# The state space stage's norm is scaled by ScalarE, with a bias that GpSimd makes

## The chip, the core and the metric

The kernel is a decoder of four layers (twelve sub-blocks, one after another) that runs as one program on one core of a Trainium2 chip. The metric is the device time of the program in microseconds. The engines' names in the profile are PE (TensorE, matmul), PEld (its weight load), DVE (VectorE), ACT (ScalarE), POOL (GpSimd) and SP (SyncE, DMA queue).

## The reference

The input x has 64 sequences of 64 tokens, 128 wide. Each sub-block adds its result to x. The change lies in the seventh, a state space model on the normalised x (`_L2_attn_ref`), with 256 channels and N = 16 states:

```python
def _layernorm(x, axis=-1, eps=1e-05):
    m = jnp.mean(x, axis=axis, keepdims=True)
    v = jnp.var(x, axis=axis, keepdims=True)
    return (x - m) / jnp.sqrt(v + eps)
...
xr = x @ w_in + b_in
xc, res = jnp.split(xr, 2, axis=-1)
u = jax.nn.silu(_causal_conv(xc, w_conv, b_conv))
A = -jnp.exp(A_log)
dt, B, C = jnp.split(u @ w_x, [DTR, DTR + N], axis=-1)
delta = jax.nn.softplus(dt @ w_dt)
deltaA = jnp.exp(delta[..., None] * A)
deltaBu = delta[..., None] * B[:, :, None, :] * u[..., None]
h = a * h + bu        # over time, for each channel and state
...
y = jnp.einsum('bldn,bln->bld', hs, C) + u * D
return y * jax.nn.silu(res) @ w_out
```

## The kernel before

The stage is `state_space` (line 2336). It works through NG = 8 groups of 512 tokens (8 sequences); group g's x lies as `e.X(g)`, 128 partitions by 4 tiles of 128 columns. After the norm and a transpose, channels are partitions: c = 0 and 1 are the two halves of the 256 channels, tokens are the 512 columns. Inside a group, k = 0 to 15 runs over the states, and m = 16 g + k counts through all of them. Each engine has a program of its own, written out in order; semaphores tie them together, and an engine that waits holds up all that stands behind in its program.

For each m, and each c: ScalarE's `decay` (line 2558, an Exp of 128x504 into PSUM) and `copy_b` (2551, the row of B from PSUM to SBUF), GpSimd's `inputs` (2616, du times that row, 128x512 each), VectorE's `scan` (2681) and then `contribute` (2688, the scan's result times the row of C), and TensorE's `accumulate` (2432) with its rows of B and C (`b_row`, `c_row`). The scan of m needs decay and input product of m; the decay of m + 1 needs the scan of m, since both use one bank. The input products are double-buffered (two m).

Between these, the steps for the groups around are placed by k. At k = 7 VectorE takes the norm's statistics of group g + 2 (`PipedNorm.stats`, 643), at k = 8 GpSimd makes 1/std from them (`rstd`, 656: an add and a power on 128x4), at k = 12 VectorE scales (`PipedNorm.scale`, 665: one TENSOR_SCALAR of 128x128 for each of the four tiles, into the one buffer `xn`). At k = 13 TensorE turns them (`turn`, 2369) and ScalarE copies the result (`copy_ln`, 2488); at k = 14 and 15 follow the input projections. For group g + 1: convolution at k = 0 to 3, at k = 5 to 10 the other projections with SiLU (k = 6), the rows of B and C (`high_part`, `below_high`, and `parts` on GpSimd at k = 9) and the step sizes; ScalarE's `softplus` (k = 11) is an Ln, which needs a table load before it and another one after it for the next Exp. At k = 12 GpSimd's `step_size` (2627) makes delta and du, two products of 128x1024. At k = 1 to 5 the output of group g - 1 is finished: `skipped` (VectorE), `gated` (GpSimd), `output` (TensorE), `residual` (VectorE, 2702). Groups 6 and 7 have no group g + 2, and so no statistics and no scale in the loop.

The norm of groups 0 and 1 and all projections of group 0 are made ahead of the loop, in a serial prologue. There ScalarE's program runs `copy_ln(0)` first, and `copy_ln(1)` right behind `copy_b(1)`.

Of the kernel before, what the change touches and what calls it, by code (L numbers as in the profile page):

```python
# [18 lines left out]
ALU = mybir.AluOpType  # L19
# [5 lines left out]
D = 128  # L25
NT = 4
# [600 lines left out]
NG = 8  # L627


class PipedNorm:  # L630
# [25 lines left out]
    def rstd(self, q, g):  # L656
        rs, mv = self.half(self.rs, g, 2 * NT), self.half(self.mv, g, 2 * NT)
        q.wait_ge(self.mean_s, g + 1)
        if g >= 2:
            q.wait_ge(self.xn_s, NT * (g - 1))  # L660
        q.tensor_scalar(rs[:, 0:NT], tiles(mv)[:, :, 1], self.eps, None, ALU.add).then_inc(self.var_s, 1)  # L661
        q.wait_ge(self.var_s, g + 1)
        q.tensor_tensor(rs[:, NT:2 * NT], rs[:, 0:NT], self.e.mhalf[:, 0:NT], ALU.pow).then_inc(self.rstd_s, 1)  # L663

    def scale(self, q, g):
        rs, mv = self.half(self.rs, g, 2 * NT), self.half(self.mv, g, 2 * NT)
# [1669 lines left out]
def state_space(nc, e, W):  # L2336
# [5 lines left out]
    M = NG * N  # L2342
    use = ssm_order()
    names = PN_SEMS + ("zeroed misc_mm misc_cp taps_done u_done res_done hi_done parts_own bc_parts relu_done sp_own sp_done "
                       "dl_done du_done b_mm c_mm b_cp a_done bu_done hs_done hc_done acc_mm yo_done yr_done")
    with block_of(nc, "state_space", names) as (block, s):
        room = Room(e.arena)
        u_b, res_b, delta_b, du_b = (room.pair(2 * GT) for _ in range(4))
# [10 lines left out]
        misc = e.bank(7)  # L2359
        at, cbank, bbank, acc = (lambda c: e.bank(c)), (lambda m: e.bank(2 + m % 2)), e.bank(4), (lambda c: e.bank(5 + c))  # L2360
        ln = PipedNorm(e, s, room, e.X, lambda g: xn, 1e-5)

        @block.tensor
        def _(pe):
# [119 lines left out]
        def _(a):  # L2484
# [3 lines left out]
            def copy_ln(g):  # L2488
                have("ln", g)
                if g >= 1:  # L2490
                    a.wait_ge(s["misc_mm"], use["m3", g - 1] + 1)
                a.activation(xnT, misc, ACT.Copy).then_inc(s["misc_cp"], 1)

            def channels(c, g):
                have(("m0", "m1")[c], g)
                if g == 0:
                    a.wait_ge(s["zeroed"], 1)
                else:
                    a.wait_ge(s["misc_mm"], use[("cv0", "cv1")[c], g - 1] + 1)
                a.activation(xp(c)[:, :, 3:3 + S], tiles(misc, NB), ACT.Identity,  # L2500
                             bias=W("b_in")[:, c:c + 1]).then_inc(s["misc_cp"], 1)
# [56 lines left out]
            def decay(m, c):  # L2558
                if m < M:
# [5 lines left out]
                    if k == 0:  # L2565
                        a.wait_ge(s["dl_done"], g + 1)
                    a.activation(tiles(at(c), NB)[:, :, 1:S], tiles(delta(g, c), NB)[:, :, 1:S], ACT.Exp,  # L2567
                                 scale=e.aneg[:, c * N + k:c * N + k + 1]).then_inc(s["a_done"], 1)

            copy_ln(0)  # L2570
            channels(0, 0)
            channels(1, 0)
# [9 lines left out]
            decay(0, 0)  # L2582
            decay(0, 1)
            copy_b(1)
            copy_ln(1)
            channels(0, 1)
            channels(1, 1)
            for m in range(M):
                g, k = m // N, m % N
                decay(m + 1, 0)  # L2590
                copy_b(m + 2)
                decay(m + 1, 1)
                if g + 1 < NG:
                    if k in (1, 3):
                        raw(("cv0", "cv1")[k // 2], g + 1)
                    if k in (5, 6):
                        raw(("m2", "m3")[k - 5], g + 1)
                    if k == 6:
                        silus(g + 1)
                    if k == 7:  # L2600
                        copy_dt(g + 1)
                    if k == 8:
                        high_part(g + 1)
                    if k in (9, 10):
                        step_size(k - 9, g + 1)
                    if k == 11:
                        softplus(g + 1)
                if g + 2 < NG:
                    if k == 13:
                        copy_ln(g + 2)  # L2610
                    if k in (14, 15):
                        channels(k - 14, g + 2)

        @block.gpsimd
        def _(q):
# [36 lines left out]
                q.tensor_copy(low, rest).then_inc(s["bc_parts"], 1)  # L2652
                q.wait_ge(s["bc_parts"], g + 1)

            ln.rstd(q, 0)
            ln.rstd(q, 1)
            parts(0, "ln_rstd", 2)
            step_size(0)
            inputs(0)
            for m in range(M):  # L2660
                g, k = m // N, m % N
                inputs(m + 1)
                if k == 2 and g >= 1:
                    gated(g - 1)
                if k == 12 and g + 1 < NG:
                    step_size(g + 1)
                if k == 9 and g + 1 < NG:
                    parts(g + 1, "bu_done", 2 * (m + 2))
                if k == 8 and g + 2 < NG:
                    ln.rstd(q, g + 2)  # L2670
            gated(NG - 1)

        @block.vector
        def _(v):
# [28 lines left out]
                v.wait_ge(s["misc_mm"], use["y", g] + 1)  # L2703
                v.tensor_tensor(e.X(g), misc, e.X(g), ALU.add).then_inc(s["misc_cp"], 1)

            def scale(g):
                if g >= 1:
                    v.wait_ge(s["misc_mm"], use["ln", g - 1] + 1)
                ln.scale(v, g)

            for c in range(2):
                v.memset(tiles(at(c), NB)[:, :, 0:1], 0.0)
            v.memset(xp_all, 0.0).then_inc(s["zeroed"], 1)
            ln.stats(v, 0)
            ln.stats(v, 1)
            scale(0)
            for c in range(2):
                for i in range(4):
                    ins = v.tensor_scalar(taps(c, i), e.ident, W("w_conv")[:, 4 * c + i:4 * c + i + 1], None, ALU.mult)
            ins.then_inc(s["taps_done"], 1)  # L2720
            scale(1)
            below_high(0)
            for m in range(M):
                g, k = m // N, m % N
# [7 lines left out]
                    below_high(g + 1)  # L2732
                scan(m, 1)
                contribute(m, 0)
                if g + 2 < NG:
                    if k == 7:
                        ln.stats(v, g + 2)
                    if k == 12:
                        scale(g + 2)
            contribute(M - 1, 1)  # L2740
            skipped(NG - 1)
            residual(NG - 1)
# [1086 lines left out]
```

## Time and profile before

| what | us |
|---|---|
| median of 3 runs | 3444.28 (3443.8 to 3452.95) |
| the profiled execution | 3446.75 |
| its span in the trace | 3444.8 |
| the state space stage in it, first memset to last residual | 1612.6 to 2226.2 |
| VectorE busy, whole kernel | 1954.5 (57% of the span) |
| TensorE / ScalarE / GpSimd busy, whole kernel | 2755.0 / 1330.5 / 1425.9 |

The profile is of one execution. The page gives each engine's busy time over the whole kernel; since the twelve stages differ, the stage is read from stretches of the trace. A timeline row gives start, duration, engine, line, instruction, operands and shapes; a row with x4 merges four neighbours; square brackets hold the idle time of the engine before it and what ended it. The name given there is inferred: where several were waited for, it is the last by the profile.

### The profile page before, as it was taken

Reading aid. Unit: us, or ns where it says so; the run is one execution under the profiler, and the core shown is the slowest. Engines: PE = TensorE matmul, PEld = TensorE weight load, DVE = VectorE, ACT = ScalarE, POOL = GpSimd, SP = SyncE. Lnnn points to the kernel's source line nnn. Section 1 sums busy time; section 2 is a strip of 40 time slices with the busy share of each in tenths; the row PEclk is TensorE's granted clock in tenths of the full one; section 3 lists DMA queues with packets and bytes.
Section 4 is the critical chain, followed back from the end, with each engine's and each line's share of the span. In section 5 each row is a group of like instructions: output and inputs, shape, how many; then the busy total and the mean of one; then the engine's idle time right before and its main releaser. Section 6 shows DMA issues by size and latency. Waiting matters only on the chain. (4 is left out here: it accounts for less than half of the span.)

```text
span 3444.8 us, 72909 instructions
## 1 busy us (share of the span) xinstructions
PE 2755.0 (80%) x28239; PEld 1918.5 (56%) x28239; DVE 1954.5 (57%) x4206; ACT 1330.5 (39%) x2252; POOL 1425.9 (41%) x1537
## 2 busy tenths in 40 slices
PE   4987784998999979786778888695777999993394
PEld 2654453996777755564233333253446888883394
DVE  2654554115767646633599898845565665644123
ACT  3432221441111124321666666352233666651153
POOL 2544443223212145253577777633452111113555
PEclk8988876999999999798899999896788999995697
DMA  6000001660000010033000000000000000001275
GB/s 230 2 1 1 1 1 43 172 175 13 3 3 3 3 46 14 1 115 121 0 1 0 1 1 0 1 1 1 1 2 11 7 7 5 5 2 45 91 230 158
DMA packets 98053, 130.50 MB, mean 38 GB/s; under 512 B 31088, under 2 KB 76528, under 8 KB 97264
## 3 DMA queue, kind: packets, MB, share of 16 engines
q1 hardware_dynamic: 82768, 109.30, 10.5%
q0 software_dynamic: 7168, 14.78, 1.2%
q8 instruction: 227, 3.72, 0.4%
q10 hardware_dynamic: 7776, 1.77, 0.2%
q14 instruction: 114, 0.93, 0.1%
HBM read 103.64 MB, written 25.35 MB: 37 GB/s over the span
## 5 line engine op out<-in xcount | busy, mean ns | idle before, releaser
L661 POOL TENSOR_SCALAR arena<-arena 128x4 f32<-128x4 f32 x120 | 27.5, 229 | 1044.4 <-DVE arena L653 794.1
L2625 POOL TENSOR_TENSOR arena<-arena 128x512 f32<-128x512 f32 x256 | 319.1, 1270 | 141.9 <-ACT arena L2556 141.2
L2686 DVE TENSOR_TENSOR_SCAN arena<-ps,arena 128x512 f32<-128x512 f32 x256 | 312.1, 1219 | 41.3 <-ACT ps L2567 22.5
L2438 PE MATMUL ps<-arena,const_w 128*128 128x512 f32 x512 | 279.2, 629 | 12.6 <-DVE arena L2694 11.5
L163 PEld LDWEIGHTS ps<-L_attn_w,arena 128*128 128x128 f32 x1984 | 241.7, 193 | 53.6 <-issue 42.5
L163 PE MATMUL ps<-L_attn_w,arena 128*128 128x128 f32 x1984 | 257.9, 281 | 8.0 <-POOL arena L2638 3.4
L2567 ACT ACTIVATE ps<-arena,aneg 128x504 f32<-128x504 f32 x256 | 174.4, 681 | 120.0 <-DVE arena L2686 119.8
L1765 PE MATMUL ps<-arena,L_attn_w 128*128 128x512 f32 x384 | 184.5, 617 | 0.9 <-ACT arena L725 0.9
L429 ACT ACTIVATE arena<-ps 128x1024 f32<-128x1024 f32 x96 | 98.3, 1024 | 223.9 <-PE ps L331 223.9
L1833 ACT ACTIVATE arena<-ps,L_attn_w 128x512 f32<-128x512 f32 x64 | 44.0, 687 | 332.6 <-PE ps L1765 332.6
L2694 DVE TENSOR_TENSOR arena<-arena,ps 128x512 f32<-128x512 f32 x256 | 170.0, 665 | 0.0
L312 PE MATMUL ps<-arena 64*64 64x512 f32 x768 | 119.2, 695 | 62.9 <-POOL arena L485 62.9
L2416 PE MATMUL ps<-bcp,sel 96*128 96x512 bf16 x256 | 92.2, 396 | 87.6 <-DVE arena L2694 67.1
L2438 PEld LDWEIGHTS ps<-arena,const_w 128*128 128x128 f32 x512 | 95.0, 198 | 99.6 <-DVE arena L2694 55.1
L423 ACT ACTIVATE arena<-arena 128x1024 f32<-128x1024 f32 x96 | 101.3, 1055 | 96.3 <-DVE arena L551 96.3
L345 PEld LDWEIGHTS ps<-arena 128*64 128x64 f32 x3072 | 108.5, 149 | 49.6 <-issue 27.6
L2229 DVE TENSOR_REDUCE arena<-arena 128x8 f32<-128x512 f32 x128 | 87.2, 681 | 84.1 <-ACT arena L2116 84.0
L2416 PEld LDWEIGHTS ps<-bcp,sel 96*128 96x128 bf16 x256 | 25.5, 100 | 195.2 <-issue 194.2
L485 POOL TENSOR_TENSOR arena<-arena,const_w 128x1024 f32<-128x1024 f32 x64 | 120.6, 1896 | 32.7 <-PE ps L319 22.9
L163 PE MATMUL ps<-L_attn_w,ct_all 128*128 128x128 f32 x1024 | 131.0, 280 | 1.9 <-DVE arena L2245 1.9
L663 POOL TENSOR_TENSOR arena<-arena,mhalf 128x4 f32<-128x4 f32 x120 | 125.4, 1045 | 10.0
L1076 DVE SCALAR_TENSOR_TENSOR arena<-ps,arena 128x64 f32 x108 | 30.7, 284 | 174.2 <-PE ps L895 165.7
(454 smaller groups left out, 6730.7 us busy)
## 6 DMA issues: line engine op xcount, KB each, us to landing
arena<-zone_w SPq DMA_DIRECT2D x54, 512.0 KB
arena<-pair_w SPq DMA_DIRECT2D x40, 578.0 KB
arena<-rt SPq DMA_DIRECT2D x24, 384.0 KB
pair_in<-pair_free SPq DMA_DIRECT2D x1, 5200.0 KB, 28.8
arena<-pair_in SPq DMA_DIRECT2D x40, 130.0 KB
arena<-ctx SPq DMA_DIRECT2D x16, 256.0 KB, 2.9
arena<-pair_out SPq DMA_DIRECT2D x16, 256.0 KB, 5.0
arena<-arena SPq DMA_DIRECT2D x108, 32.0 KB, 2.2
```

Source lines behind the costliest of these rows:

```text
L163: ins = pe.matmul(out, src[:, j * P:(j + 1) * P], w, start=(i == 0), stop=(bias is None and i == len(chunks) - 1))
L312: ins = pe.matmul(tile(b2, h), q(g)[rows, t:t + S], kbd(i)[rows, :, b2 * S:(b2 + 1) * S], start=True, stop=rope)
L345: ins = pe.matmul(obank[b2 * S:(b2 + 1) * S, hp], pts(i)[:, hp * P + b2 * S:hp * P + (b2 + 1) * S], vbd(g)[:, 2 * j + b2, hp], start=True, ...
L485: p_.tensor_tensor(kbd(i), repeat(k(g)[:, j * P:(j + 1) * P], HH), spread(e.hmask8, P), ALU.mult).then_inc(s["kbd_done"], 1)
L663: q.tensor_tensor(rs[:, NT:2 * NT], rs[:, 0:NT], self.e.mhalf[:, 0:NT], ALU.pow).then_inc(self.rstd_s, 1)
L1765: pe.matmul(e.bank(i), W(w)[:, col], xnT(g), start=True, stop=True).then_inc(s["qkg_mm"], 1)
L2416: return pe.matmul(out, e.sel[:, row:row + 1].broadcast_to([96, P]), bcp(g), start=True, stop=True)
L2438: pe.matmul(acc(c), e.ident, hc(m, c), start=(k == 0), stop=(k == N - 1)).then_inc(s["acc_mm"], 1)
L2567: a.activation(tiles(at(c), NB)[:, :, 1:S], tiles(delta(g, c), NB)[:, :, 1:S], ACT.Exp, scale=e.aneg[:, c * N + k:c * N + k + 1]).then_inc ...
L2625: q.tensor_tensor(bu(m, c), du(g, c), bs(m), ALU.mult).then_inc(s["bu_done"], 1)
L2686: v.tensor_tensor_scan(hs(m, c), at(c), bu(m, c), 0.0, ALU.mult, ALU.add).then_inc(s["hs_done"], 1)
L2694: v.tensor_tensor(hc(m, c), hs(m, c), cbank(m), ALU.mult).then_inc(s["hc_done"], 1)
```

## The change

VectorE's `scale` is gone from the stage. `PipedNorm.offset` is new: GpSimd multiplies mean and 1/std (128x4) and negates the product, each step waiting for the one before; it is called right behind each `rstd`. `PipedNorm.scale_act` is new: ScalarE computes x * rs + nb, an Identity activation of 128x128 for each tile with scale and bias from SBUF. Calls stand on ScalarE ahead of `copy_ln(0)`, behind `copy_b(1)`, and at k = 12 for group g + 2, behind the decays of the next k. The statistics stay on VectorE. In the changed file lines are shifted; TensorE's program is the same.

```diff
--- before.py
+++ after.py
@@ -662,6 +662,23 @@
         q.wait_ge(self.var_s, g + 1)
         q.tensor_tensor(rs[:, NT:2 * NT], rs[:, 0:NT], self.e.mhalf[:, 0:NT], ALU.pow).then_inc(self.rstd_s, 1)
 
+    def offset(self, q, g, nb, raw, sem):
+
+        rs, mv = self.half(self.rs, g, 2 * NT), self.half(self.mv, g, 2 * NT)
+        q.wait_ge(self.rstd_s, g + 1)
+        if g >= 2:
+            q.wait_ge(self.xn_s, NT * (g - 1))
+        q.tensor_tensor(nb, tiles(mv)[:, :, 0], rs[:, NT:2 * NT], ALU.mult).then_inc(raw, 1)
+        q.wait_ge(raw, g + 1)
+        q.tensor_scalar(nb, nb, -1.0, None, ALU.mult).then_inc(sem, 1)
+        q.wait_ge(sem, g + 1)
+
+    def scale_act(self, a, g, nb):
+        rs = self.half(self.rs, g, 2 * NT)
+        for j in range(NT):
+            a.activation(self.dst(g)[:, j * self.step:j * self.step + D], self.src(g)[:, j * D:(j + 1) * D], ACT.Identity,
+                         bias=nb[:, j:j + 1], scale=rs[:, NT + j:NT + j + 1]).then_inc(self.xn_s, 1)
+
     def scale(self, q, g):
         rs, mv = self.half(self.rs, g, 2 * NT), self.half(self.mv, g, 2 * NT)
         q.wait_ge(self.mean_s, g + 1)
@@ -2342,7 +2359,7 @@
     M = NG * N
     use = ssm_order()
     names = PN_SEMS + ("zeroed misc_mm misc_cp taps_done u_done res_done hi_done parts_own bc_parts relu_done sp_own sp_done "
-                       "dl_done du_done b_mm c_mm b_cp a_done bu_done hs_done hc_done acc_mm yo_done yr_done")
+                       "nb_raw nb_done dl_done du_done b_mm c_mm b_cp a_done bu_done hs_done hc_done acc_mm yo_done yr_done")
     with block_of(nc, "state_space", names) as (block, s):
         room = Room(e.arena)
         u_b, res_b, delta_b, du_b = (room.pair(2 * GT) for _ in range(4))
@@ -2359,6 +2376,7 @@
         misc = e.bank(7)
         at, cbank, bbank, acc = (lambda c: e.bank(c)), (lambda m: e.bank(2 + m % 2)), e.bank(4), (lambda c: e.bank(5 + c))
         ln = PipedNorm(e, s, room, e.X, lambda g: xn, 1e-5)
+        nb = room.pair(NT)
 
         @block.tensor
         def _(pe):
@@ -2491,6 +2509,12 @@
                     a.wait_ge(s["misc_mm"], use["m3", g - 1] + 1)
                 a.activation(xnT, misc, ACT.Copy).then_inc(s["misc_cp"], 1)
 
+            def scale(g):
+                a.wait_ge(s["nb_done"], g + 1)
+                if g >= 1:
+                    a.wait_ge(s["misc_mm"], use["ln", g - 1] + 1)
+                ln.scale_act(a, g, nb(g))
+
             def channels(c, g):
                 have(("m0", "m1")[c], g)
                 if g == 0:
@@ -2567,6 +2591,7 @@
                     a.activation(tiles(at(c), NB)[:, :, 1:S], tiles(delta(g, c), NB)[:, :, 1:S], ACT.Exp,
                                  scale=e.aneg[:, c * N + k:c * N + k + 1]).then_inc(s["a_done"], 1)
 
+            scale(0)
             copy_ln(0)
             channels(0, 0)
             channels(1, 0)
@@ -2582,6 +2607,7 @@
             decay(0, 0)
             decay(0, 1)
             copy_b(1)
+            scale(1)
             copy_ln(1)
             channels(0, 1)
             channels(1, 1)
@@ -2606,6 +2632,8 @@
                     if k == 11:
                         softplus(g + 1)
                 if g + 2 < NG:
+                    if k == 12:
+                        scale(g + 2)
                     if k == 13:
                         copy_ln(g + 2)
                     if k in (14, 15):
@@ -2652,8 +2680,9 @@
                 q.tensor_copy(low, rest).then_inc(s["bc_parts"], 1)
                 q.wait_ge(s["bc_parts"], g + 1)
 
-            ln.rstd(q, 0)
-            ln.rstd(q, 1)
+            for g in range(2):
+                ln.rstd(q, g)
+                ln.offset(q, g, nb(g), s["nb_raw"], s["nb_done"])
             parts(0, "ln_rstd", 2)
             step_size(0)
             inputs(0)
@@ -2668,6 +2697,7 @@
                     parts(g + 1, "bu_done", 2 * (m + 2))
                 if k == 8 and g + 2 < NG:
                     ln.rstd(q, g + 2)
+                    ln.offset(q, g + 2, nb(g + 2), s["nb_raw"], s["nb_done"])
             gated(NG - 1)
 
         @block.vector
@@ -2703,22 +2733,15 @@
                 v.wait_ge(s["misc_mm"], use["y", g] + 1)
                 v.tensor_tensor(e.X(g), misc, e.X(g), ALU.add).then_inc(s["misc_cp"], 1)
 
-            def scale(g):
-                if g >= 1:
-                    v.wait_ge(s["misc_mm"], use["ln", g - 1] + 1)
-                ln.scale(v, g)
-
             for c in range(2):
                 v.memset(tiles(at(c), NB)[:, :, 0:1], 0.0)
             v.memset(xp_all, 0.0).then_inc(s["zeroed"], 1)
             ln.stats(v, 0)
             ln.stats(v, 1)
-            scale(0)
             for c in range(2):
                 for i in range(4):
                     ins = v.tensor_scalar(taps(c, i), e.ident, W("w_conv")[:, 4 * c + i:4 * c + i + 1], None, ALU.mult)
             ins.then_inc(s["taps_done"], 1)
-            scale(1)
             below_high(0)
             for m in range(M):
                 g, k = m // N, m % N
@@ -2732,11 +2755,8 @@
                     below_high(g + 1)
                 scan(m, 1)
                 contribute(m, 0)
-                if g + 2 < NG:
-                    if k == 7:
-                        ln.stats(v, g + 2)
-                    if k == 12:
-                        scale(g + 2)
+                if g + 2 < NG and k == 7:
+                    ln.stats(v, g + 2)
             contribute(M - 1, 1)
             skipped(NG - 1)
             residual(NG - 1)
```

ScalarE's program at the end of k = 11 and in k = 12 to 13 of a group, before. L2549 is softplus's Ln, L2567 the decays, L2556 `copy_b`, L2492 `copy_ln`:

```order
830 L2549 ACT_TABLE_LOAD
831 L2549 ACTIVATE arena<-arena 128x1024
832 L2567 ACT_TABLE_LOAD
833 L2567 ACTIVATE ps<-arena,aneg 128x8x63
834 L2556 ACTIVATE arena<-ps 128x512
835 L2567 ACTIVATE ps<-arena,aneg 128x8x63 x2
836 L2556 ACTIVATE arena<-ps 128x512
837 L2567 ACTIVATE ps<-arena,aneg 128x8x63
838 L2492 ACTIVATE arena<-ps 128x512
```

The same place now; L2573, L2591, L2580 and L2510 are those four lines, L679 is the new scale:

```order
834 L2573 ACT_TABLE_LOAD
835 L2573 ACTIVATE arena<-arena 128x1024
836 L2591 ACT_TABLE_LOAD
837 L2591 ACTIVATE ps<-arena,aneg 128x8x63
838 L2580 ACTIVATE arena<-ps 128x512
839 L2591 ACTIVATE ps<-arena,aneg 128x8x63
840 L679 ACTIVATE arena<-x_all,arena 128x128 x4
841 L2591 ACTIVATE ps<-arena,aneg 128x8x63
842 L2580 ACTIVATE arena<-ps 128x512
843 L2591 ACTIVATE ps<-arena,aneg 128x8x63
844 L2510 ACTIVATE arena<-ps 128x512
```

Four activations now stand between the second decay of k = 13 and the first of k = 14; no table load has been added. On GpSimd, from k = 8 to `step_size` of k = 12, before (L661 and L663 are `rstd`, L2625 the input products, L2647 to L2652 `parts`, L2630 `step_size`):

```order
983 L661 TENSOR_SCALAR arena<-arena 128x4
984 L663 TENSOR_TENSOR arena<-arena,mhalf 128x4
985 L2625 TENSOR_TENSOR arena<-arena 128x512 x2
986 L2647 CAST bcp<-arena 32x512
987 L2648 CAST bcm<-arena 32x512
988 L2650 TENSOR_TENSOR arena<-arena,bcm 32x512
989 L2652 CAST bcp<-arena 32x512
990 L2625 TENSOR_TENSOR arena<-arena 128x512 x6
991 L2630 TENSOR_TENSOR arena<-arena 128x1024
```

The same place now, with the offset's product (L671) and negation (L673):

```order
987 L661 TENSOR_SCALAR arena<-arena 128x4
988 L663 TENSOR_TENSOR arena<-arena,mhalf 128x4
989 L671 TENSOR_TENSOR arena<-arena 128x4
990 L673 TENSOR_SCALAR arena<-arena 128x4
991 L2653 TENSOR_TENSOR arena<-arena 128x512 x2
992 L2675 CAST bcp<-arena 32x512
```

Two small instructions have come ahead of the input products of k = 10 and of `parts`.

## Rows read from the trace of the kernel before

**Rows 1.** Stretches: from:to, length, busy PE, PEld, DVE, ACT, POOL, clock, DMA.

```profile
1805.00:1875.00 70.00, 57.16 (x151) 22.88 (x150) 64.52 (x80) 45.41 (x69) 51.07 (x41) 0.93 0.00 0
```

**Rows 2.** Waits of VectorE in the stage: total us, times, longest.

```profile
DVE arena L2686 <- ACT ps L2567: 22.5, 12, 3.2
```

**Rows 3.** Timeline (start, us, engine) of VectorE, group 2, k = 12 to 14.

```profile
1860.97 1.22 DVE L2686 TENSOR_TENSOR_SCAN arena<-ps,arena 128x512 f32<-128x512 f32 x1
...
1862.68 6.27 DVE L670 TENSOR_SCALAR arena<-x_all,arena 128x128 f32<-128x128 f32 x4
1868.87 1.21 DVE L2686 TENSOR_TENSOR_SCAN arena<-ps,arena 128x512 f32<-128x512 f32 x1
...
1872.29 1.21 DVE L2686 TENSOR_TENSOR_SCAN arena<-ps,arena 128x512 f32<-128x512 f32 x1
```

**Rows 4.** Timeline of the other engines at the same place, group 2.

```profile
1862.82 2.40 POOL L2630 TENSOR_TENSOR arena<-arena 128x1024 f32<-128x1024 f32 x1 [0.52 <-ACT arena L2549]
1863.99 0.69 ACT L2567 ACTIVATE ps<-arena,aneg 128x504 f32<-128x504 f32 x1
...
1865.09 0.68 ACT L2567 ACTIVATE ps<-arena,aneg 128x504 f32<-128x504 f32 x1
...
1867.61 2.48 POOL L2625 TENSOR_TENSOR arena<-arena 128x512 f32<-128x512 f32 x2
...
1871.19 1.91 PE L2438 MATMUL ps<-arena,const_w 128*128 128x512 f32 x2
```

**Rows 5.** Timeline of group 6, k = 12 to 14: VectorE, then ScalarE, then GpSimd.

```profile
2144.20 1.22 DVE L2686 TENSOR_TENSOR_SCAN arena<-ps,arena 128x512 f32<-128x512 f32 x1
...
2147.94 1.22 DVE L2686 TENSOR_TENSOR_SCAN arena<-ps,arena 128x512 f32<-128x512 f32 x1 [1.94 <-ACT ps L2567]
...
2152.14 1.22 DVE L2686 TENSOR_TENSOR_SCAN arena<-ps,arena 128x512 f32<-128x512 f32 x1 [0.69 <-ACT ps L2567]
...
2149.20 0.69 ACT L2567 ACTIVATE ps<-arena,aneg 128x504 f32<-128x504 f32 x1 [0.20 <-DVE arena L2686]
...
2150.79 9.86 POOL L2625 TENSOR_TENSOR arena<-arena 128x512 f32<-128x512 f32 x8
```

**Rows 6.** Timeline of VectorE: the residuals of groups 4, 5 and 6.

```profile
2042.55 0.69 DVE L2704 TENSOR_TENSOR x_all<-ps,x_all 128x512 f32<-128x512 f32 x1 [2.83 <-PE ps L163]
...
2113.13 0.69 DVE L2704 TENSOR_TENSOR x_all<-ps,x_all 128x512 f32<-128x512 f32 x1 [2.83 <-PE ps L163]
...
2179.02 0.69 DVE L2704 TENSOR_TENSOR x_all<-ps,x_all 128x512 f32<-128x512 f32 x1 [1.49 <-PE ps L163]
```

**Rows 7.** Timeline of the prologue, group 0.

```profile
1615.38 1.05 POOL L663 TENSOR_TENSOR arena<-arena,mhalf 128x4 f32<-128x4 f32 x1
...
1616.54 1.12 DVE L670 TENSOR_SCALAR arena<-x_all,arena 128x128 f32<-128x128 f32 x4 [0.39 <-POOL arena L663]
...
1618.23 0.60 ACT L2492 ACTIVATE arena<-ps 128x512 f32<-128x512 f32 x1 [25.24 <-PE ps L2373]
```

**Rows 8.** Timeline of the last stage: GpSimd, then ScalarE.

```profile
3408.83 1.04 POOL L663 TENSOR_TENSOR arena<-arena,mhalf 128x4 f32<-128x4 f32 x1
...
3410.23 0.25 POOL L1644 TENSOR_SCALAR arena<-arena 128x4 f32<-128x4 f32 x1
...
3410.51 1.65 ACT L1610 ACTIVATE arena<-arena 128x128 f32<-128x128 f32 x4 [17.60 <-POOL arena L1644]
```

**Rows 9.** Timeline of group 2 at k = 11: GpSimd's inputs, VectorE's scan.

```profile
1854.23 4.95 POOL L2625 TENSOR_TENSOR arena<-arena 128x512 f32<-128x512 f32 x4
...
1855.62 1.22 DVE L2686 TENSOR_TENSOR_SCAN arena<-ps,arena 128x512 f32<-128x512 f32 x1
```

**Rows 10.** Timeline of the prologue, group 1, and the first wait of the loop.

```profile
1663.37 1.06 PE L2373 MATMUL ps<-const_w,arena 128*128 128x128 f32 x4
...
1667.52 0.58 ACT L2492 ACTIVATE arena<-ps 128x512 f32<-128x512 f32 x1
...
1674.48 1.22 DVE L2686 TENSOR_TENSOR_SCAN arena<-ps,arena 128x512 f32<-128x512 f32 x1 [3.09 <-ACT ps L2567]
```

## The prediction, made before the changed kernel was run

> **What bounds the kernel now.** First the stretches of the state space stage: in a typical 70 us VectorE is busy for 64.5, TensorE for 57.2, GpSimd for 51.1 and ScalarE for 45.4 [rows 1]. Then VectorE's waits: for the decays of its scans only 22.5 us in the whole stage [rows 2]; otherwise it runs scan and product in turn, two pairs in 1872.29 - 1868.87 = 3.42 us [rows 3]. So the stage ends when VectorE ends, and an edit is worth what it moves VectorE's scans. Below, k = 0 to 15 are the sixteen states of a group of 512 tokens, and there are eight groups.
>
> Last the scale itself. Its four VectorE instructions take 1.12 us in the prologue, but 6.27 us inside the loop [rows 3, 7]. While they run, GpSimd is in the two wide products of `step_size` and the first input product of k = 14 [rows 4]. Groups 0 to 5 each have one, 6.26 or 6.27 us long.
>
> **Part 1, the scales leave VectorE in the loop (six times).** The naive gain is 6 x 6.27 = 37.6 us. It isn't all to be had, since others are late behind those 6.27 us. Group 6 is the control that the trace itself holds: at k = 12 it does `step_size` for group 7, but has no scale. There VectorE waits 1.94 us for the decay of k = 13 (ScalarE had to load a table, take a logarithm and load again), then 0.69 us before the scan of k = 14 [rows 5]. The trace names ScalarE for the 0.69, but that decay was over at 2149.20 + 0.69 = 2149.89; what ended last, at 2150.79 + 1.27 = 2152.06, is GpSimd's first product of k = 14, which had queued behind `step_size` (9.86 us for eight of them, 1.27 a piece by the single ones) [rows 5]. From the second scan of k = 12 to the first of k = 14 it is 2152.14 - 2144.20 = 7.94 us in group 6, and 1872.29 - 1860.97 = 11.32 us in group 2 with the scale [rows 3, 5]. **The gain is 3.38 us a group**, not 6.27. By hand in group 2 itself: the decay of k = 13 ends at 1864.68, so its scan starts at 1864.75 instead of 1868.87; the first product of k = 14 ends at 1867.61 + 1.27 = 1868.88, so that scan starts at 1868.95 instead of 1872.29, 3.34 earlier [rows 3, 4]. A check over a longer distance: residual to residual takes 70.58 us from group 4 to 5 and 65.89 from 5 to 6 with the control between; of the 4.69 less, 1.34 is a shorter wait for the output (1.49 against 2.83), which leaves 3.35 [rows 6]. Sum: 6 x 3.38 = **20.3 us** less.
>
> The rows show 6.27 us for four scales beside a busy GpSimd, 1.12 beside a nearly free one [rows 3, 7]. A rule of the Trainium skill speaks against the change: Perfetto Trace Analysis, Optimizing Scalar/DVE Operations, says that where VectorE has a performance mode for an operation, it is faster there than on ScalarE. By that rule alone the scales would cost VectorE 1.12 us a group, less than the 1.94 us that it would wait for the decay anyway, so the loop would gain nothing and the sum would be that of rival E. The 6.27 us decide against it. The reason that fits stands in SBUF — State Buffer, Who interferes with whom: such an instruction and one of GpSimd exclude each other for a whole instruction; the trace agrees in that the four scales last about as long as the two wide products and the input product beside them.
>
> **Part 2, ScalarE gets them.** The last stage of the kernel has exactly this instruction, an Identity of 128x128 with bias and scale from SBUF: four take 1.65 us [rows 8]. At k = 12 they stand behind the second decay of k = 13 and ahead of the first of k = 14. In group 2: 1865.77 + 1.65 = 1867.4 [rows 4]. The decay of k = 14 needs the scan of k = 13, over at 1865.97; it starts 1.4 us late, ends at 1868.1, and its scan can't start before 1868.95 for GpSimd's sake. Slack 0.8. Next `copy_b` for k = 15 ends at 1868.7, and GpSimd is free for it only at 1868.88 + 1.27 = 1870.1. So ScalarE's 6 x 1.65 us are hidden by `step_size`; without that cover they would cost 1.4 us a group. TensorE's transposes (k = 13) come behind an accumulation that needs VectorE's product of 1866.5, so they start near 1868.3 and not later for the scale's sake; `copy_ln` follows near 1869.5, and the decay of k = 15, needed at 1872.4, near 1871. If TensorE is as slow there as at 1871.19 (1.91 us for a pair of 512-column matmuls [rows 4]), the decays of k = 15 or 16 come up to 0.7 us late. Bounds per group: 2.7 to 3.6 us gained, the upper one 0.2 above the control, which is how far such checks differ among each other. I take 3.38, the row of the control.
>
> **Part 3, GpSimd's offset.** A product and a negation of 128x4, each waiting for the one before it. In the last stage the same pair is over 0.64 us behind the end of the power (3408.83 + 1.04 = 3409.87 to 3410.51) [rows 8]. From k = 8 on GpSimd works without a gap (rstd, inputs of 10, `parts`, inputs of 11), and the first product of k = 11 ends at 1854.23 + 1.27 = 1855.50, where its scan starts at 1855.62 [rows 9]. So VectorE comes some 0.5 us late at k = 11. But the next thing that it needs from elsewhere is the decay of k = 13, which stands behind two table loads and not behind VectorE: the wait of 1.94 shrinks. Cost 0 in the sum; without that cover 6 x 0.6 = 3.6 us.
>
> **Part 4, the prologue.** Here all is serial. Group 0: VectorE's scale began 0.11 us after the power (1615.38 + 1.05 to 1616.54) and took 1.12 us; now it begins 0.64 after and takes 1.65: 0.53 + 0.53 = **1.1 us** more before `copy_ln(0)` and all behind it [rows 7, 8]. It may be 1.6, as GpSimd's small instructions can meet VectorE's eight tap products, which move up by 1.3 us into the scale's place; the taps are due only at the convolution, long after, so that their earlier place is worth nothing. Group 1: before, the transposes were done by 1664.4 and `copy_ln(1)` ran at 1667.52, right behind `copy_b(1)`. Now scale(1) stands in that place: 1.65 us, and 0.57 us from the last scale to `copy_ln`, as in the prologue of before (1617.66 to 1618.23): **2.2 us** more [rows 7, 10]. All of it shows, since VectorE waited 3.09 us at 1674.48 for a decay behind that chain [rows 10]. Bounds 1.2 (if half of it finds slack further down) to 2.6.
>
> **Sum** against the profiled execution's own 3446.75 us: -20.3 + 1.1 + 2.2 = -17.0, so 3429.7. The median of the runs shown is 2.5 us below that execution, which gives 3427.3. Forecast **3427.5 us**, 0.5% less. Its own bounds: -(6 x 3.6) + 1.1 + 1.2 = -19.3 and -(6 x 2.7) + 1.6 + 2.6 = -12.0, so 3425 to 3432.3.
>
> **The rivals.**
>
> A, all of the 6.27 comes back: 37.6 - 3.3 = 34.3 us less, 3410. For it: VectorE is the busiest engine. Against: group 6.
>
> B, the offset isn't absorbed: 3.6 us more than forecast, 3431. For: GpSimd has no slack at k = 11. Against: the wait at k = 13.
>
> C, ScalarE is late after all: the queue of decay, `copy_b`, decay runs 1.4 us behind from k = 14 on; 6 x 1.4 = 8.4 us, 3436. For: ScalarE works strictly in order, and the slack is only 0.8. Against: each step by hand above.
>
> D, slower than before: `copy_ln` stands on ScalarE waiting for TensorE's transposes, with the decays of k = 15 behind it. Before, the normalised rows were ready well ahead of the transposes; now only 1 us. If the transposes slip behind the next accumulation, VectorE waits for ScalarE, and TensorE for VectorE. This decides from 17.0 / 6 = 2.8 us a group on; at 4.5 us it is 6 x 4.5 - 17 = +10, 3454. Against: by the steps above 0.7 at most.
>
> E, a scale is cheap on VectorE (1.12 us for four, were the 6.27 not its own): the loop gains nothing and the prologue loses 3.3, 3447.6. This is where the first page named above leads.
>
> **Chances.** Forecast 0.65, A 0.04, B 0.12, C 0.13, D 0.04, E 0.02. About 0.3% (10.3 us) is what a measurement of this kernel can tell from no change. Faster by more than that are the forecast, A and B, 0.81, less 0.02 for a tail of the forecast: 0.79. Within: C, E and that tail, 0.17. Slower: D, 0.04. The range takes in the forecast's bounds, B and C, and 4 us on the fast side for a gain above the control's: 3421 to 3437.
>
> **What would show it.** Right: no TENSOR_SCALAR of VectorE in the loop; in groups 0 to 6 alike a wait of 1.3 to 1.9 us before the scan of k = 13 and of some 0.7 before that of k = 14; residual to residual near 67.2 us; 1.65 us of ScalarE for each four scales; the wait of 3.09 grown to some 5.3. Wrong: waits of over 1 us at k = 15 or 16 (C, D), a wait at k = 11 that isn't given back at k = 13 (B), no wait at k = 13 (A).

## The result, and the profile after

| | median us | runs | ratio to before (95%) |
|---|---|---|---|
| before | 3446.41 | 5 (3443.8 to 3452.95) | |
| changed kernel | 3429.31 | 5 (3426.24 to 3431.69) | 0.9942 (0.9931 to 0.9954) |
| changed kernel, second comparison | 3426.65 | 6, against 3441.4 | 0.9955 (0.9943 to 0.9967) |
| changed kernel, third comparison | 3434.22 | 5, against 3447.29 | 0.9954 (0.9941 to 0.9968) |

By the medians the kernel is 17.1 us faster in the first comparison, 14.8 and 13.1 in the other two; the ratios make it 20, 15.5 and 15.9. The forecast was 17.0 less, which lies within all three intervals; as a time it was 3427.5 us, 1.8 below what was measured. The five runs of the kernel before include the three of the table of the time before.

First VectorE's timeline of the changed kernel at the place of [rows 3], group 2. The columns are start, duration, engine, line; L2716 is the scan.

```profile
1843.88 1.22 DVE L2716 TENSOR_TENSOR_SCAN arena<-ps,arena 128x512 f32<-128x512 f32 x1 [2.02 <-ACT ps L2591]
...
1856.25 1.22 DVE L2716 TENSOR_TENSOR_SCAN arena<-ps,arena 128x512 f32<-128x512 f32 x1 [0.75 <-ACT ps L2591]
...
1861.39 1.21 DVE L2716 TENSOR_TENSOR_SCAN arena<-ps,arena 128x512 f32<-128x512 f32 x1
...
1864.49 1.23 DVE L2716 TENSOR_TENSOR_SCAN arena<-ps,arena 128x512 f32<-128x512 f32 x1 [1.31 <-ACT ps L2591]
...
1868.70 1.22 DVE L2716 TENSOR_TENSOR_SCAN arena<-ps,arena 128x512 f32<-128x512 f32 x1 [0.70 <-issue]
```

From the second scan of k = 12 to the first of k = 14: 1868.70 - 1861.39 = 7.31 us where [rows 3] had 11.32 and the control of [rows 5] 7.94. Of that gain, 0.75 us has been given back a little ahead, by a new wait at k = 11 (before, the scan of k = 11 began without one [rows 9]). So three waits stand where one block of 6.27 us stood: 0.75, 1.31 and 0.70.

Then ScalarE and GpSimd in the same stretch (L679 is the scale, L2658 and L2661 `step_size`, L2653 the input products):

```profile
1865.48 1.64 ACT L679 ACTIVATE arena<-x_all,arena 128x128 f32<-128x128 f32 x4
1867.02 0.67 ACT L2591 ACTIVATE ps<-arena,aneg 128x504 f32<-128x504 f32 x1
...
1869.58 0.60 ACT L2510 ACTIVATE arena<-ps 128x512 f32<-128x512 f32 x1 [0.80 <-PE ps L2391]
...
1854.89 7.42 POOL L2653 TENSOR_TENSOR arena<-arena 128x512 f32<-128x512 f32 x6
1862.61 2.35 POOL L2658 TENSOR_TENSOR arena<-arena 128x1024 f32<-128x1024 f32 x1 [0.30 <-ACT arena L2573]
1865.03 2.35 POOL L2661 TENSOR_TENSOR arena<-arena 128x1024 f32<-128x1024 f32 x1
1867.35 9.89 POOL L2653 TENSOR_TENSOR arena<-arena 128x512 f32<-128x512 f32 x8
```

The four activations take 1.64 us. The decay of k = 14 behind them is over at 1867.69. The first product of k = 14 is over only at 1867.35 + 1.27 = 1868.62, right before the scan of 1868.70. The wait of 0.75 reads the same way: the row names ScalarE, but the first product of k = 11 ended at 1854.89 + 1.27 = 1856.16, and the scan began at 1856.25.

The residuals of the changed kernel, which answer to [rows 6], are evenly spaced, 67.20 us here where it was 70.6 to 71.2:

```profile
1829.70 0.69 DVE L2734 TENSOR_TENSOR x_all<-ps,x_all 128x512 f32<-128x512 f32 x1 [2.83 <-PE ps L163]
...
1896.90 0.69 DVE L2734 TENSOR_TENSOR x_all<-ps,x_all 128x512 f32<-128x512 f32 x1 [2.83 <-PE ps L163]
```

The prologue, in answer to [rows 7] and [rows 10]:

```profile
1622.82 1.17 POOL L663 TENSOR_TENSOR arena<-arena,mhalf 128x4 f32<-128x4 f32 x1
...
1624.07 0.33 POOL L671 TENSOR_TENSOR arena<-arena 128x4 f32<-128x4 f32 x1
...
1624.49 0.48 POOL L673 TENSOR_SCALAR arena<-arena 128x4 f32<-128x4 f32 x1
1625.01 1.65 ACT L679 ACTIVATE arena<-x_all,arena 128x128 f32<-128x128 f32 x4 [24.82 <-POOL arena L673]
...
1627.22 0.60 ACT L2510 ACTIVATE arena<-ps 128x512 f32<-128x512 f32 x1 [0.57 <-PE ps L2391]
...
1680.21 1.22 DVE L2716 TENSOR_TENSOR_SCAN arena<-ps,arena 128x512 f32<-128x512 f32 x1 [5.28 <-ACT ps L2591]
```

The first copy comes 7.20 us after the stage's first memset (1620.02) where it came 5.65 after it (1612.58): 1.55 us later. GpSimd's small instructions were stretched to 1.17, 0.33 and 0.48 us beside VectorE's taps, against 1.04, 0.20 and 0.25 in the last stage [rows 8]; in this same prologue, for group 1, when the taps were over, they took 1.04, 0.20 and 0.25 too. The wait for the decay of k = 1 is 5.28 us where it was 3.09.

To place the whole gain, the stage is cut at the starts of VectorE's instructions (us). The profiles of the experiments below are used too, except e5, e6 and e8, whose loops do other work; their first column is 51.89, 51.89 and 50.34:

| kernel | first memset to first scan | first scan to scan of k = 1 | from there to last residual |
|---|---|---|---|
| before (4 profiles) | 55.79, 55.92, 55.87, 50.35 | 6.11, 6.11, 6.11, 6.10 | 551.01, 549.94, 551.34, 552.52 |
| changed (3 profiles) | 51.88, 51.87, 57.32 | 8.31, 8.32, 8.32 | 531.56, 532.19, 531.81 |
| e3, loop only | 50.33 | 6.12 | 531.65 |
| e4, prologue only | 51.69 | 8.31 | 551.58 |
| e7 and e11, VectorE at k = 7 | 50.35, 50.36 | 6.10, 6.11 | 531.98, 530.09 |

The first column has two levels in either kernel, 5.5 us apart. That is told under the experiments. At the shorter level, the change costs 51.88 - 50.34 = 1.5 us there, and 2.2 in the second column. The third, by the means of the first two rows, gains 551.2 - 531.9 = 19.3. Sum: -15.6 us in the stage. Outside the stage the program varies by more than these differences: the first memset stands anywhere from 1606.5 to 1623.9 us in these profiles, although nothing ahead of it was edited. So small differences are read from the stage, not from the time.

### The profile page after: what moved, and what is told of

Same layout as the page of the kernel before. It is cut to its first block and busy times, and to the rows that moved or that the text cites. A ratio compares the mean times of both kernels' runs of the same rounds, so it can differ in the third digit from the quotient of the medians.

```text
span 3428.8 us, 72931 instructions
## 1 busy us (share of the span) xinstructions
PE 2747.4 (80%) x28239; PEld 1910.0 (56%) x28239; DVE 1912.3 (56%) x4174; ACT 1343.0 (39%) x2284; POOL 1431.3 (42%) x1553
## 5 line engine op out<-in xcount | busy, mean ns | idle before, releaser
L661 POOL TENSOR_SCALAR arena<-arena 128x4 f32<-128x4 f32 x120 | 27.7, 231 | 1039.6 <-DVE arena L653 788.8
L2653 POOL TENSOR_TENSOR arena<-arena 128x512 f32<-128x512 f32 x256 | 318.6, 1273 | 121.2 <-ACT arena L2580 120.0
L2716 DVE TENSOR_TENSOR_SCAN arena<-ps,arena 128x512 f32<-128x512 f32 x256 | 310.9, 1215 | 58.4 <-ACT ps L2591 37.4
L2456 PE MATMUL ps<-arena,const_w 128*128 128x512 f32 x512 | 272.2, 614 | 13.5 <-DVE arena L2724 12.3
L2591 ACT ACTIVATE ps<-arena,aneg 128x504 f32<-128x504 f32 x256 | 174.3, 681 | 103.7 <-DVE arena L2716 103.5
L2434 PE MATMUL ps<-bcp,sel 96*128 96x512 bf16 x256 | 93.6, 387 | 71.6 <-DVE arena L2724 55.9
L663 POOL TENSOR_TENSOR arena<-arena,mhalf 128x4 f32<-128x4 f32 x120 | 125.4, 1045 | 10.0
L687 POOL TENSOR_SCALAR arena<-x_all,arena 128x128 f32<-128x128 f32 x160 | 125.8, 799 | 7.3 <-POOL arena L663 6.2
```

What stands on the lines that cost most here:

```text
L687: q.tensor_scalar(self.dst(g)[:, j * self.step:j * self.step + D], self.src(g)[:, j * D:(j + 1) * D], mv[:, 2 * j:2 * j + 1], rs[:, NT + j ...
L2456: pe.matmul(acc(c), e.ident, hc(m, c), start=(k == 0), stop=(k == N - 1)).then_inc(s["acc_mm"], 1)
L2653: q.tensor_tensor(bu(m, c), du(g, c), bs(m), ALU.mult).then_inc(s["bu_done"], 1)
L2716: v.tensor_tensor_scan(hs(m, c), at(c), bu(m, c), 0.0, ALU.mult, ALU.add).then_inc(s["hs_done"], 1)
```

## The experiments

**The kernel before, again (e1, e9, e10; no edit).** The first pair of profiles had the stage 21.1 us shorter, 4 more than forecast, and a faster prologue where a slower one was foreseen.

> The kernel before, once more. The stage is read from its first memset on VectorE to the first VectorE instruction of the next stage: 614.5 us in the profile before, 593.4 in the one after. Of these 21.1 us, 17.0 were foreseen; the prologue to the first scan took 55.8 us before and 51.9 after, although it had 1.1 us more to do, because TensorE's granted clock was 0.50 in two stretches before where it was 0.97 to 1.00 after. Theory P (the clock in the prologue falls by execution, not by the change): this new profile of the same kernel may show either, so the prologue lies anywhere from 50 to 56 us, and the loop from the scan of k = 1 to the last residual is again 551.0 +- 0.5. Theory Q (the change sets the clock): prologue again 55.8 +- 0.3. Time against the kernel before: 1.000.

> The kernel before, a third profile. Open is the prologue: 55.8 and 55.9 us from the first memset to the first scan in two profiles of it, 50.3 in three profiles of kernels whose prologue has the same instructions (e3, e7, e8). Theory P (by execution, not by kernel): after two slow ones, a third and a fourth profile show 50.3 us at least once. Theory R (something fixed in this program sets it): 55.8 again in both. The loop from the scan of k = 1 to the last residual is 550 to 551 us in either case.

> The kernel before, a fourth profile: as for the third. P: 50.3 us in at least one of the two; R: 55.8 in both.

Measured: ratios to before 0.9993 (0.9985 to 1.0002) for e1, single runs of 3447.03 and 3448.67 us for e9 and e10. Their prologues took 55.92, 55.87 and 50.35 us. So the same program shows both levels. TensorE's rows part them. Two stretches of the first profile, whose stage began at 1612.58 (columns as in [rows 1]; the clock is the last number but two):

```profile
1632.00:1642.00 10.00, 6.43 (x13) 2.18 (x14) 0.00 (x0) 3.86 (x5) 0.00 (x0) 0.92 0.00 1
1642.00:1652.00 10.00, 7.92 (x10) 1.50 (x8) 0.69 (x1) 1.39 (x3) 1.09 (x2) 0.50 0.00 1
```

And about the same work in the profile of the changed kernel, whose stage began at 1620.02:

```profile
1639.00:1649.00 10.00, 6.36 (x13) 2.02 (x12) 0.00 (x0) 3.24 (x5) 0.00 (x0) 1.00 0.00 0
1649.00:1659.00 10.00, 6.03 (x12) 1.41 (x12) 0.69 (x1) 3.78 (x6) 2.96 (x4) 0.97 0.00 1
```

The granted clock was 0.50, the lower of its two levels (1.2 GHz), from 30 us into the stage in the one, and 0.97 of full speed (2.4 GHz) in the other. Ahead of that both ran the convolution's matmuls and two pairs of projections with pauses of 0.78 us for ScalarE, and then paused 2.02 us for the SiLUs; the four matmuls of 128x512 behind that pause took 3.65 us in the kernel before and 1.90 in the changed one. Theory P stands: the level changes between executions, and the change isn't needed for either level, since e10 had the short prologue without it and e12 the long one with it (57.32 us). That both kernels meet the two levels equally often is not shown: it was the long one in 3 of 4 profiles of the kernel before, in 1 of 3 of the changed kernel, and in none of the seven profiles of the other kernels. How much of a difference of medians is due to that stays open; the loop's column is free of it.

**The changed kernel, again (e2, e12; no edit).**

> The changed kernel, once more, beside e1 on one chip. Loop from the scan of k = 1 to the last residual 531.6 +- 0.5 us in any case. Theory P: prologue to the first scan anywhere from 51.5 to 57.5. Theory Q: again 51.9 +- 0.3. Time 17 us less than before (0.9951) by P, 21 us less (0.9939) by Q.

> The changed kernel, a third time, beside the kernel with the scale at k = 7: 17 us less than before, with 19.4 of them in the loop; stage 593.4 to 594.0 us, prologue to the first scan 51.9, as in the five profiles of kernels with this prologue (P: one of them may be slower).

Measured: 0.9955 and 0.9954, loops 532.19 and 531.81 us, prologues 51.87 and 57.32, the second 5.4 us above the 51.9 expected (the case that P left open). The loop is the same each time, and its gain is the change's.

**The loop's part alone (e3).** The prologue's scales go back to VectorE:

```diff
-            scale(0)
             copy_ln(0)
...
-            scale(1)
             copy_ln(1)
...
-            for g in range(2):
-                ln.rstd(q, g)
-                ln.offset(q, g, nb(g), s["nb_raw"], s["nb_done"])
+            ln.rstd(q, 0)
+            ln.rstd(q, 1)
...
             ln.stats(v, 1)
+            scale(0)
...
             ins.then_inc(s["taps_done"], 1)
+            scale(1)
```

> Only the six scales of the loop go to ScalarE (with their offsets on GpSimd); groups 0 and 1 are scaled by VectorE as before. My theory: the loop's gain is whole and the prologue's cost of 1.1 + 2.2 us is gone: 20.3 us less than before, 3.3 less than the changed kernel; the wait of VectorE for the decay of k = 1 is 3.1 us again, and the loop from there to the last residual is as in the changed kernel, 531.6. Rival (the gain in the prologue comes from the change): the stage is not shorter than the changed kernel's 593.4.

Measured: 3423.61 us, 0.9948 (0.9934 to 0.9962), 17.8 us less than before where 20.3 were expected (the interval takes that in), and 3.0 less than the 3426.65 of the changed kernel. The trace is the sharper measure: loop 531.65, the wait at k = 1 back at 3.09, the prologue 50.33. The stage took 589.7 us against 593.4, so the rival fell.

**The prologue's part alone (e4).** ScalarE scales groups 0 and 1, VectorE the rest as before:

```diff
                 if g + 2 < NG:
-                    if k == 12:
-                        scale(g + 2)
                     if k == 13:
                         copy_ln(g + 2)
...
                     ln.rstd(q, g + 2)
-                    ln.offset(q, g + 2, nb(g + 2), s["nb_raw"], s["nb_done"])
...
+                    if k == 12:
+                        scale(g + 2)
```

> The other part alone: groups 0 and 1 are scaled by ScalarE, the loop by VectorE as before. My theory: slower than before by 1.1 to 1.6 us up to ScalarE's first copy and 2.2 us at group 1, 3.3 to 3.8 in all (1.001); the wait for the decay of k = 1 is 5.3 us, the loop from there is 551.0. Rival (the change's prologue is the faster one, by TensorE's clock): 3 to 4 us faster than before.

Measured: 3445.69 us against 3441.4, 1.0017 (1.0008 to 1.0026), slower by some 4 to 6 us; by the trace 1.35 us up to the first scan (51.69 against 50.34) and 2.2 at k = 1, 3.6 in all. The changed kernel had 1.5 in the first place: here GpSimd's small instructions met the taps a little differently (1.05, 0.26 and 0.48 us). The rival falls. The two parts are separate and add up.

**GpSimd's offset twice (e5).**

```diff
+        if g >= 2:
+            q.tensor_scalar(nb, nb, -1.0, None, ALU.mult).then_inc(again, 1)
+            q.wait_ge(again, 2 * (g - 2) + 1)
+            q.tensor_tensor(nb, tiles(mv)[:, :, 0], rs[:, NT:2 * NT], ALU.mult).then_inc(again, 1)
+            q.wait_ge(again, 2 * (g - 2) + 2)
         q.tensor_scalar(nb, nb, -1.0, None, ALU.mult).then_inc(sem, 1)
```

> The changed kernel with GpSimd's negation and product done once more in the loop (0.6 us more a group at k = 8). My theory (the offset is absorbed by the wait for the decay of k = 13): the wait at k = 11 grows from 0.73 to about 1.3 us, the one at k = 13 shrinks from 1.33 to about 0.7, residual to residual stays at 67.2 us, and the time is the changed kernel's. Rival (the offset costs what it lasts): 0.6 us more a group, residual to residual 67.8, 3.6 us in all.

Measured: 0.9958 (0.9941 to 0.9974) and residual to residual 67.6 us where the changed kernel has 67.23, between the two theories. VectorE's waits at k = 11 and 13, then ScalarE's second decay of k = 12:

```profile
1861.14 1.22 DVE L2721 TENSOR_TENSOR_SCAN arena<-ps,arena 128x512 f32<-128x512 f32 x1 [1.32 <-issue]
...
1869.19 1.22 DVE L2721 TENSOR_TENSOR_SCAN arena<-ps,arena 128x512 f32<-128x512 f32 x1 [1.12 <-ACT ps L2596]
...
1864.11 0.69 ACT L2596 ACTIVATE ps<-arena,aneg 128x504 f32<-128x504 f32 x1 [0.27 <-DVE arena L2721]
```

The first wait grew by 0.57, as both said, but the second shrank by 0.19 only. The reason is in the last row: ahead of the logarithm ScalarE has the second decay of k = 12 to do, and that waits for VectorE's second scan of k = 11. In the changed kernel the decay began 0.24 us after that scan (1859.18 to 1859.42), here 0.03 after it (1864.08 to 1864.11), so some 0.2 us was to spare. GpSimd had little more room: ahead of `step_size` it waited 0.30 us for the logarithm in the changed kernel, and in e5 its row shows no wait. So the cover of Part 3 is thin: it held for one offset (residual to residual 67.23 us, and 67.21 in e7, which has none), and not for a second.

**ScalarE's scale twice (e6).**

```diff
+        if g >= 2:
+            for j in range(NT):
+                a.activation(spare[:, j * D:(j + 1) * D], self.src(g)[:, j * D:(j + 1) * D], ACT.Identity,
+                             bias=nb[:, j:j + 1], scale=rs[:, NT + j:NT + j + 1])
         for j in range(NT):
```

> The changed kernel with four more activations of the same kind ahead of the scale at k = 12 (written to a spare buffer), 1.65 us more of ScalarE a group. My theory: the slack behind GpSimd's product of k = 14 is 1.0 us (decay over at 1867.7, scan at 1868.7), so VectorE comes 0.65 us later a group: residual to residual 67.9, 3.9 us in all. Rival 1 (ScalarE's work is free, since it is idle for a third of the stage): 0. Rival 2 (ScalarE's order holds everything up): 1.65 a group, 9.9 us.

Measured: 0.9954 (0.994 to 0.9969), residual to residual 67.77 us, 0.54 a group more where 0.65 was expected; the time alone doesn't part it from the changed kernel, the trace does. The wait before the scan of k = 14:

```profile
1868.17 1.22 DVE L2721 TENSOR_TENSOR_SCAN arena<-ps,arena 128x512 f32<-128x512 f32 x1 [1.25 <-ACT ps L2596]
```

It was 0.70, and 0.55 of ScalarE's extra 1.54 us (1864.39 to 1865.93) show. ScalarE had 1.0 us to spare here; not more, although it is idle for a third of the stage. Both rivals fell.

**VectorE scales where GpSimd is idle (e7, e11).** Based on the kernel before:

```diff
+                if k == 5 and g + 2 < NG:
+                    ln.stats(v, g + 2)
                 if k == 5 and g >= 1:
                     residual(g - 1)
...
-                if g + 2 < NG:
-                    if k == 7:
-                        ln.stats(v, g + 2)
-                    if k == 12:
-                        scale(g + 2)
+                if g + 2 < NG and k == 7:
+                    scale(g + 2)
...
-                if k == 8 and g + 2 < NG:
+                if k == 5 and g + 2 < NG:
                     ln.rstd(q, g + 2)
```

> Based on the kernel before: VectorE keeps the scale, but at k = 7, where it waits 3.2 us for the SiLUs and GpSimd is idle; the statistics move to k = 5, ahead of the residual for which VectorE waits 2.8 us, and rstd to k = 5. No work for ScalarE and no offset. My theory (the price of 6.27 us came from GpSimd's wide products beside it, and the gain from having nothing of VectorE's at k = 12): the four scales take 1.1 to 2.5 us instead of 6.27 and hide in the wait; the stage's loop is as short as the changed kernel's, and the prologue is as before: 20.3 us less than before, about 3.3 less than the changed kernel. Rival (the scale costs 6.27 us on VectorE by itself): some 3 us a group stick out of the wait, so that only 2 to 5 us are gained in all.

> The kernel with VectorE's scale at k = 7, once more, on one chip beside the changed kernel. By the first profile the stage is 590.1 us against 593.4 to 594.0 of the changed kernel: 3.3 to 3.9 us less in the time. If the first comparison (25 us less than before) holds, 8 us less than the changed kernel.

Measured: 0.9926 (0.9913 to 0.9938) and 0.9947 (0.9933 to 0.996), that is 24.8 us less than before by the medians in the first comparison and 16.1 in the second. In the second it took 3431.18 us beside 3434.22 for the changed kernel: 3 us less, not the 8 that were expected if the first held. VectorE and GpSimd at the new place:

```profile
1835.33 1.11 DVE L670 TENSOR_SCALAR arena<-x_all,arena 128x128 f32<-128x128 f32 x4
1838.63 1.22 DVE L2686 TENSOR_TENSOR_SCAN arena<-ps,arena 128x512 f32<-128x512 f32 x1 [2.19 <-ACT ps L2567]
...
1839.19 3.74 POOL L2625 TENSOR_TENSOR arena<-arena 128x512 f32<-128x512 f32 x3 [5.67 <-ACT arena L2556]
...
1859.25 1.22 DVE L2686 TENSOR_TENSOR_SCAN arena<-ps,arena 128x512 f32<-128x512 f32 x1 [1.94 <-ACT ps L2567]
1863.46 1.22 DVE L2686 TENSOR_TENSOR_SCAN arena<-ps,arena 128x512 f32<-128x512 f32 x1 [0.69 <-ACT ps L2567]
```

Four scales take 1.11 us while GpSimd is idle for 5.67, and lie whole in the wait for the SiLUs. (The statistics have left that wait for the one ahead of the residual; this run moves both, and does not part their shares.) At k = 13 and 14 stand exactly the waits of the control, 1.94 and 0.69 [rows 5]. Residual to residual is 67.2 us, as in the changed kernel, with nothing added to ScalarE or GpSimd and the prologue as it was. By the trace the stage, up to the next one's first VectorE instruction, took 590.0 us in e7 and 588.2 in e11, against 593.4 and 594.0 in the changed kernel at the same level of the prologue. e7's 3.7 us are about what the change costs in the prologue; e11's further 1.9 us lie mostly in the last group (45.9 us from residual to residual where e7 has 47.6). In the times the three us lie within the spread of the runs, so this version is at least as good as the changed kernel, and better by the trace.

**Half of GpSimd's step_size (e8).**

```diff
-                q.tensor_tensor(delta_b(g), delta_b(g), du_b(g), ALU.add).then_inc(s["dl_done"], 1)
+                d, p, x = ((t[:, 0:GT] if g >= 1 else t) for t in (delta_b(g), du_b(g), u_b(g)))
+                q.tensor_tensor(d, d, p, ALU.add).then_inc(s["dl_done"], 1)
...
-                q.tensor_tensor(du_b(g), delta_b(g), u_b(g), ALU.mult).then_inc(s["du_done"], 1)
+                q.tensor_tensor(p, d, x, ALU.mult).then_inc(s["du_done"], 1)
```

> The kernel before, with GpSimd's step_size of groups 1 to 7 done for the first half of the channels only (two products of 128x512 instead of 128x1024; delta and du of the other half are left wrong, so that work is left out). The scale stays on VectorE at k = 12. My theory: each of the four scales waits for a GpSimd instruction, so four take about 1.27 x 3 + 0.34 = 4.2 us instead of 6.27. Rival: 6.27 still, if the duration belongs to the instruction itself.

Measured, VectorE and then GpSimd:

```profile
1855.38 4.11 DVE L670 TENSOR_SCALAR arena<-x_all,arena 128x128 f32<-128x128 f32 x4
...
1855.52 1.33 POOL L2631 TENSOR_TENSOR arena<-arena 128x512 f32<-128x512 f32 x1 [0.51 <-ACT arena L2549]
1856.92 1.27 POOL L2634 TENSOR_TENSOR arena<-arena 128x512 f32<-128x512 f32 x1
1858.15 2.48 POOL L2625 TENSOR_TENSOR arena<-arena 128x512 f32<-128x512 f32 x2
```

4.11 us where 4.2 was expected, and residual to residual 68.4 us, shorter than before by the same 2.2 us as the scales. The same four instructions take 1.11, 4.11 or 6.27 us, and the difference is what GpSimd does beside them: nothing, three products of 128x512, or two of 128x1024 and one of 128x512. That VectorE's two-port instructions and GpSimd's block one another for whole instructions is what the Trainium skill says (SBUF — State Buffer, Who interferes with whom), and these three numbers agree. That the scales are of that kind no run shows by itself.

## Why the prediction was right

**What bounds the stage** held: VectorE's scans set it before and after; in the changed kernel VectorE is still the busiest engine, 61.2 of 70 us (1800 to 1870), TensorE now close behind with 59.4.

**Part 1**, 20.3 us: the trace gives 19.3 by the means of the last column above. The group with a control was the right measure of a gain that stood in no single row. The naive 37.6 us (rival A) fell as the control said it would, since decay and input products are late behind the scale. The 1 us that is missing lies in group 0 (its part from k = 1 to the first residual became 82.25 us instead of 84.84, 2.6 less and not 3.4) and in the last group, which by the means took 0.8 us longer. There, the time from residual to residual varies from 45.9 to 47.6 us among profiles of the kernel before as well. The five groups between gained a little more than foreseen, 17.5 us or 3.50 each: most take 70.6 us before, which gives the 3.38 of the control, but every profile of the kernel before has one or two of 70.8 to 71.4. Why is open.

**Part 2**, ScalarE's work hidden: held, with a slack of 1.0 us where 0.8 was worked out, and measured by e6. Rivals C and D fell: there is no wait at k = 15 or 16. The waits named as signs stand in groups 0 to 5 alike (1.31 to 1.33 us at k = 13, 0.70 to 0.72 at k = 14), and in group 6, without a scale, they are 1.95 and 0.69.

**Part 3**, the offset absorbed: held in its sum (67.23 us a group against 67.21 without any offset), by a margin that the prediction had wrong. VectorE came 0.83 us late at k = 11, not 0.5 (12.37 us from the first scan of k = 8, where it was 11.54), and the wait at k = 13 gave 0.63 of it back (1.31 instead of 1.94); the rest came from a pause of 0.20 us at k = 12 that is gone. The prediction also said that the decay of k = 13 stands behind table loads and not behind VectorE. It stands behind the second decay of k = 12 too, which does wait for VectorE, and some 0.2 us was all the room. Rival B decides just beyond that, as e5 shows with 0.4 us a group.

**Part 4**, the prologue: 2.2 us at group 1 foreseen and measured (8.31 against 6.11). Group 0 was put at 1.1 with an upper bound of 1.6, and 1.55 came to the first copy (1.36 in e4). The term was sized from the last stage, where no taps run beside GpSimd's small instructions; here the taps, moved into the scale's place, stretched them by 0.13, 0.13 and 0.23 us.

**The sum**: -15.6 us by the trace of the stage, -17.1, -14.8 and -13.1 by the medians, -20, -15.5 and -15.9 by the ratios, -17.0 foreseen. The terms are right to about 1 us each. That the first medians met the sum to 0.1 us is luck. The first pair of profiles alone would have flattered it, with -21.1 us in the stage, of which 5.5 were TensorE's clock in the prologue. Rival E fell: VectorE was fast at this operation only where GpSimd let it be. The Trainium skill (Perfetto Trace Analysis, Optimizing Scalar/DVE Operations) has such an operation faster on VectorE where there is a performance mode, and adds that moving work to ScalarE may make sense where VectorE is saturated. The first holds for the slot of e7, with 1.11 us against 1.64 on ScalarE, and not for k = 12, with 6.27; there the move paid.

## What to carry to other kernels

An instruction that is slow in one place and fast in another is a question of its neighbour, and before it is moved to another engine it is worth a look whether another slot on its own engine has an idle neighbour: here a slot with a wait of 3.2 us took it for nothing, once the statistics had left it for another wait, and spared both the other engines and the prologue. When a step leaves a loop's busiest engine, look for an iteration of the same loop that lacks it already, and read the gain from that; the step's own duration was almost twice what came back. And a slack read at one step has to be followed through the in-order programs: the decay that "doesn't depend" on VectorE stood behind one that did, with some 0.2 us to spare.

## What the runs showed that was not expected

TensorE's granted clock in the serial prologue changes between executions of the same program: over 30 to 40 us from the first memset it was 0.50 in three profiles of the kernel before and 0.86 in the fourth, with a prologue of 55.8 to 55.9 us or 50.35. It was so in the changed kernel too (57.32 or 51.88 us). What had gone before it was the same row of matmuls with short pauses; the convolution's first half took 6.40 to 6.59 us in the four profiles with the long prologue, and 6.07 (e7), 5.76 (changed kernel) and 5.55 (e8) in three with the short one. In the kernel before, the clock over 10 to 20 us was 0.60 to 0.62 in the three long ones and 0.67 in the short one, so that it had risen later where it fell again later on. What decides it in an execution stays open. A difference of 5 us in one pair of profiles proves nothing about a change of this size.

A wait's named releaser misled in two places, both times in the same way. The 0.69 us of [rows 5] and the 0.75 us of the changed kernel name ScalarE, though GpSimd's product had ended 0.08 and 0.09 us before the scan, and the decay that the scan needs 2.25 and 2.26 us before it.
